# Register loads of block numbers and pair steps moved behind the last use of the numbers they replace

## The reference

```python
# layer 0: two attention convolutions over edges (src -> dst) plus one loop edge per node
xs = (x @ lin_w.T).reshape(N, H, C)                      # H = 8 heads, C = 16
alpha = a_src[src] + a_dst[dst] + a_edge                 # per edge and head
alpha = jnp.where(alpha > 0, alpha, 0.2 * alpha)
alpha = jnp.exp(alpha - segment_max(alpha, dst)[dst])
out = segment_sum(xs[src] * alpha / segment_sum(alpha, dst)[dst], dst)
h = layer_norm(elu(out + bias) + h_previous)             # twice, then a linear layer over h0, h1, h2
# a_edge comes from a small network on x[src].x[dst], |x[src]-x[dst]|^2, |x[src]|^2, |x[dst]|^2
x = _layernorm(x + layer0)
# layer 1: messages and a gated update
em = relu(layer_norm([x[src], x[dst]] @ msg_w + msg_b)) * edge_weights[:, None]
messages = segment_sum(em, dst) / (counts + 1e-8) * (counts > 0)
h_new = relu(layer_norm([x, messages] @ upd_w + upd_b))
x = _layernorm(x + gate * h_new + (1 - gate) * x)        # gate = sigmoid(x @ gate_w + gate_b)
```

## Time and profile before

| what | value |
|---|---|
| median of 3 runs | 6742.71 us |
| the profiled execution's own time | 6751.64 us |
| its span, first to last instruction | 6749.8 us |
| TensorE busy | 5088.3 us (75%) |
| VectorE busy | 4557.2 us (68%) |
| GpSimd busy | 4633.8 us (69%) |
| mean granted TensorE clock | 0.816 of full speed |
| DMA | 534.92 MB, mean 79 GB/s |

### The profile page before, as it was taken

How to read it: one execution, slowest core, us unless ns; L and a number is a source line. 1 busy time by engine, 2 the same in 40 slices (tenths; PEclk the granted TensorE clock), 3 DMA queues, 4 the chain that set the end, 5 groups by cost and what they waited for, 6 DMA issues and landing times. The chain is left out here.

```text
span 6749.8 us, 124645 instructions
## 1 busy us (share of the span) xinstructions
PE 5088.3 (75%) x33726; PEld 4548.7 (67%) x33726; DVE 4557.2 (68%) x15714; ACT 2984.2 (44%) x10333; POOL 4633.8 (69%) x4875
## 2 busy tenths in 40 slices
PE   5788888887887378888888888866666776676775
PEld 4666666676666267777777787756666666666664
DVE  5677777777777746665666666575666666666667
ACT  3344444444444322222222222255666666666666
POOL 4777777777775077777777777706777777777771
PEclk7788888888888656666666667678999999999997
DMA  8544444444443322222222222222222222222221
GB/s 174 151 115 115 114 115 115 114 113 114 115 113 84 104 61 62 63 63 63 62 63 63 62 64 63 62 85 59 54 54 54 54 54 54 54 54 54 54 54 30
DMA packets 334709, 534.92 MB, mean 79 GB/s; under 512 B 105502, under 2 KB 222767, under 8 KB 333665
## 3 DMA queue, kind: packets, MB, share of 16 engines
q0 software_dynamic: 181264, 439.20, 25.7%
q1 hardware_dynamic: 143462, 83.65, 4.6%
q10 hardware_dynamic: 9323, 4.08, 0.3%
HBM read 489.59 MB, written 42.61 MB: 79 GB/s over the span
## 5 line engine op out<-in xcount | busy, mean ns | idle before, releaser
L931 POOL DMA_INDIRECT arena<-rows,slot_src x3222 | 3086.2, 958 | 1028.1 <-issue 934.9
L723 POOL DMA_INDIRECT arena<-msg_rows,slot_src x1611 | 1523.3, 946 | 525.0 <-issue 485.5
L1129 ACT ACTIVATE arena<-psum 128x512 f32<-128x512 bf16 x808 | 480.5, 595 | 1521.4 <-PE psum L977 1518.3
L2033 PE MATMUL psum<-arena 128*128 x3232 | 700.6, 301 | 506.7 <-DMA arena<-msg_rows,slot_src 443.6
L1018 PE MATMUL psum<-arena 128*128 128x145 f32 x3232 | 978.0, 394 | 0.0
L1267 DVE TENSOR_TENSOR arena<-arena,psum 128x290 f32 x1616 | 731.3, 453 | 287.7 <-DVE arena L1267 182.3
L2033 PEld LDWEIGHTS psum<-arena 128*128 128x128 f32 x3232 | 521.3, 203 | 571.0 <-issue 570.5
L1020 PE MATMUL psum<-arena 128*128 128x145 f32 x3232 | 872.7, 361 | 0.0
L2040 ACT ACTIVATE arena<-psum 128x128 bf16<-128x128 f32 x1616 | 425.4, 277 | 753.4 <-PE psum L2035 753.0
L1204 DVE TENSOR_TENSOR arena<-arena,psum 128x512 f32<-128x512 f32 x808 | 553.5, 685 | 267.4 <-PE psum L1020 261.9
L1033 PE MATMUL psum<-arena 128*128 x3232 | 598.8, 327 | 163.7 <-ACT arena L1129 71.9
(11 more groups left out here) (360 smaller groups left out, 9567.8 us busy)
## 6 DMA issues: line engine op xcount, KB each, us to landing
arena<-rows,slot_src POOLq DMA_INDIRECT x3222
arena<-msg_rows,slot_src POOLq DMA_INDIRECT x1611
arena<-slot_keys SPq DMA_DIRECT2D x100, 128.0 KB
edge_alpha<-arena SPq DMA_DIRECT2D x50, 128.0 KB, 1.9
arena<-edge_alpha SPq DMA_DIRECT2D x50, 128.0 KB
slot_keys<-lane_keys SPq DMA_DIRECT2D x24, 256.0 KB
arena<-rows SPq DMA_DIRECT2D x6, 1024.0 KB, 10.0
rows<-arena SPq DMA_DIRECT2D x4, 822.0 KB
```

The costliest lines, as they stand in the source:

```text
L723: pool.indirect_dma_start(out=self.buffer[:, v % U, j, :], out_offset=None, in_=self.source, in_offset=bass.IndirectOffsetOnAxis(ap=K.SRC[ ...
L931: pool.indirect_dma_start(out=E.rowbuf[:, r, j, :], out_offset=None, in_=E.source, in_offset=bass.IndirectOffsetOnAxis(ap=K.SRC[:, at:at + ...
L1129: act.activation(E.onehotT[:, v % 2, :, :], E.psT, ACT.Copy).then_inc(E.turned, 1)
L2033: pe.matmul(psH[b][:, j, :], onehotT[:, b, j, :], K.by_dst[:, bass.ds(blocks(v, j), 1), :].rearrange("p b w -> p (b w)"), start=True, stop ...
```

## The change

All register loads stay, in number and content, and each moves to an earlier place in its engine's order: behind the last instruction that uses the eight numbers which it replaces, instead of in front of the first that needs the new ones. The first load of each table stands ahead of the loop.

```diff
@@ edge_pe
         v = t + 1
-        if 0 <= v < VISITS and v * G % LOADED == 0:
-            blocks = numbers_loaded(K, ET.PE, K.slot_blocks, v * G, NB - 1)
+        if v == 0:
+            blocks = numbers_loaded(K, ET.PE, K.slot_blocks, 0, NB - 1)
+            steps = numbers_loaded(K, ET.PE, K.pair_steps, 0, AW)
         near = G - 1 if E.first else G
...
             edge_select(E, v, G - 1, blocks[(v * G + G - 1) % LOADED]).then_inc(E.selected, 1)
+        if 0 <= v < VISITS - 1 and (v + 1) * G % LOADED == 0:
+            blocks = numbers_loaded(K, ET.PE, K.slot_blocks, (v + 1) * G, NB - 1)
 
         u = t + 1 - BEHIND
         if 0 <= u < VISITS:
-            if u * 2 % LOADED == 0:
-                steps = numbers_loaded(K, ET.PE, K.pair_steps, u * 2, AW)
...
                           ).then_inc(E.scattered, 1)
+            if u < VISITS - 1 and (u + 1) * 2 % LOADED == 0:
+                steps = numbers_loaded(K, ET.PE, K.pair_steps, (u + 1) * 2, AW)
@@ edge_dve
     dve, K = E.K.dve, E.K
+    blocks = numbers_loaded(K, ET.DVE, K.pair_blocks, 0, NB - 1)
...
         u = t - 17
         if 0 <= u < VISITS:
-            if u * 2 % LOADED == 0:
-                blocks = numbers_loaded(K, ET.DVE, K.pair_blocks, u * 2, NB - 1)
             for k in range(2):
                 block = blocks[(u * 2 + k) % LOADED]
...
                 edge_add(E, u, k, block)
+            if u < VISITS - 1 and (u + 1) * 2 % LOADED == 0:
+                blocks = numbers_loaded(K, ET.DVE, K.pair_blocks, (u + 1) * 2, NB - 1)
@@ message_pass
     pe_blocks[0] = numbers_loaded(K, ET.PE, K.slot_blocks, 0, NB - 1)
+    dve_blocks[0] = numbers_loaded(K, ET.DVE, K.slot_blocks, 0, NB - 1)
     for v in (0, 1):
         sums(0, v, lambda _, j: blocks_pe(v, j))
+    pe_blocks[1] = numbers_loaded(K, ET.PE, K.slot_blocks, LOADED, NB - 1)
...
-            if (at + 2) * G % LOADED == 0 and at + 2 < VISITS:
-                pe_blocks[(at + 2) * G // LOADED] = numbers_loaded(K, ET.PE, K.slot_blocks, (at + 2) * G, NB - 1)
-            if at * G % LOADED == 0:
-                dve_blocks[at * G // LOADED] = numbers_loaded(K, ET.DVE, K.slot_blocks, at * G, NB - 1)
...
                 sums(i, v + 2, lambda _, j: blocks_pe(at + 2, j))
+            if (at + 3) * G % LOADED == 0 and at + 3 < VISITS:
+                pe_blocks[(at + 3) * G // LOADED] = numbers_loaded(K, ET.PE, K.slot_blocks, (at + 3) * G, NB - 1)
             ready.wait(pe, i, v)
...
+            if (at + 1) * G % LOADED == 0 and at + 1 < VISITS:
+                dve_blocks[(at + 1) * G // LOADED] = numbers_loaded(K, ET.DVE, K.slot_blocks, (at + 1) * G, NB - 1)
```

## The result

The changed kernel takes 6816.79 us (median of 5 runs, 6809.19 to 6832.79), the kernel before 6747.60 us beside it (5 runs, 6740.57 to 6750.45): ratio 1.0106, 95% interval 1.0095 to 1.0117. It is 69 us slower. The forecast, 6890 us, had the sign and the place right and about twice the size.

The account below looks back on a forecast made before the run. GpSimd's gathers bound the messages and second pass, the TensorE-VectorE loop the first. First pass +141 us (+2.1 per period, 106, plus clock 35), second +5, messages +1, total +147: 6890 us, range 6775 to 7040.

Parts of the forecast that it names:

- New holes at u mod 8 = 2 and 6: First pass, u the visit scattered: slot loads newly between selects and scatter cost +1.0 and +1.7 us per eight visits.
- VectorE's loads: First pass: moved behind the second add, partly hidden by the mult's wait for the scatter; -0.85 and -0.37 us per period.
- the clock: First pass: more holes raise TensorE's half-speed share from 0.24 to 0.35; 0.7 us per period, 35 us (0 to 100).
- the pair-step loads: First pass: twice per period, now behind the scatter, in front of transposes and selects; 0.35 us each, +0.7 (0 to 3.8).
- the old stalls: First pass: the slot loads' stalls at their old place, mostly not reaching VectorE; -0.1 us per period (down to 0.7).
- TensorE's issue waits in front of the scatter: Sign of being right: in the first pass their count grows from 41 to over 120 in the same stretch.
- Mult waits grow from 209.8: Sign of being right: VectorE's mult waits for the scatter total more than 209.8 us in the first pass's stretch.
- Gathers further apart in the first pass only, clock under 0.88: Sign of being right: GpSimd's gathers exceed 1.276 us spacing in the first pass only, whose clock falls under 0.88.
- A, the loads hide: Rival, chance 0.10: loads disappear behind queued work, the first pass reaches GpSimd's pace and gains 41 us; 6702 us.
- The cap of 41 us: First pass: most a faster loop can win before GpSimd's 1.250 us per gather binds, 1611 gathers x 0.026.
- C, the second pass: Rival, chance 0.13: second pass's clock stays at half, TensorE becomes the bound, 141 us more; 7031 us.
- The messages: Message pass: TensorE's load moves in front of the scatter, GpSimd keeps its pace; +1 us (0 to 5) for the tail.

Follow-up runs that it names:

- e5: Kernel before with only TensorE's slot loads of the two attention passes moved behind the fourth select, undisturbed chip: 7145.12 us, ratio 1.0593.
- e8: Kernel before with pair-step loads moved behind the scatter and VectorE's loads behind the second add, slot loads unmoved, undisturbed chip: 6715.54 us, ratio 0.9957.
- e12: Changed kernel without pair-step reloads (loaded once per attention pass), chip with late releases: 8165.18 us, ratio 0.9944 to the kernel before.
- e6: Kernel before with only the pair-step loads moved behind the transposes, in front of the selects, undisturbed chip: 6713.86 us, ratio 0.9957.
- e7: Kernel before with each table loaded once per attention pass and never reloaded, so sums go to wrong blocks, undisturbed chip: 6686.94 us, ratio 0.9912.
- e11: Kernel before with only VectorE's pair-block loads moved behind the second add of the visit before, chip with late releases: 8208.14 us, ratio 0.9995.
- e1: Kernel before with only TensorE's slot loads of the attention passes moved behind the fourth select, chip with late releases: 8293.20 us, ratio 1.0090.

## Why the prediction was right in kind and twice too large

**The place.** The loop between TensorE and VectorE sets the pace of the first pass, the slot loads between selects and scatter lengthen it, the other passes don't move. All shown: by the pass lengths, by e5, and by e8, which takes the slot loads out of the change and turns +1.06% into -0.43%. How the total divides among the terms is in part bookkeeping, as said below.

**The terms.** Per period of eight visits the first pass went from 1700 / (1333 / 32) = 40.8 us to 1700 / (1280 / 32) = 42.5 us, by the 1333 and 1280 gathers in 400 to 2100: +1.7, where the prediction had +2.8. I put each mult of that stretch into its place in the period and averaged its wait, for e5 as well:

| wait of the mult for the scatter, us | u mod 8 = 0 | 1 | 2 | 4 | 6 | sum |
|---|---|---|---|---|---|---|
| before | 3.37 | 0 | 0 | 1.0 | 0.6 | 5.0 |
| after | 1.54 | 0.2 | 0.69 | 0 | 2.71 | 5.1 |
| e5 | 5.72 | 0 | 0.75 | 3.57 | 2.79 | 12.8 |

- New holes at u mod 8 = 2 and 6: predicted 1.0 + 1.7 = 2.7. The waits there rose by 0.7 and 2.1, together 2.8; in e5, where VectorE's loads are unmoved, by 0.75 and 2.2, together 2.9. Right.
- VectorE's loads: predicted -0.85 - 0.37 = -1.2. The waits at 0 and 4 fell by 1.8 and 1.0; VectorE's visible load rose from 71.8 / 41.7 = 1.7 us to 60.8 / 40 + (77.4 - 9.5) / 40 = 3.2 us, 9.5 us being what the take's issue waits were before. -2.8 + 1.5 = -1.3. Right, by the trace's accounts; no run took this edit alone on an undisturbed chip. One can read the same numbers as a rival: the mult's waits hardly changed in sum (5.0 and 5.1 us), and the 1.5 us that VectorE's load shows more are nearly all of the lengthening. For the reading by places speaks e5: its two single holes alone give 2.9 us, more than the whole 1.7, so something else in the change must win back over 1 us. That it is VectorE's load, no run on an undisturbed chip separates.
- What is left, 1.7 - 2.8 + 1.3 = +0.2 us, is the clock, the pair-step loads and the old stalls together. Predicted 0.7 + 0.7 - 0.1 = +1.3. These are the terms of the sum that were mis-sized, the pair-step loads and the clock: 1.1 us, 56 us over 50.5 periods, of the 59 us by which the first pass and its forecast differ (82 against 141).
- Of it, the clock: I let the share at half speed rise from 0.24 to 0.35; it rose to 0.28 (0.86). At my own price, 3 x 0.04 x 2.2 = 0.26 us and 13 us for the pass, not 35.
- The pair-step load, then, is left with about zero, not 0.7. That is a remainder and not a measurement. The 1.26 us hole in front of the transposes at 1514.18 is real, and in the trace ScalarE waits 1.16 us for them, until 1514.60; but the selects behind them end at 1515.61, and VectorE's take, held by its own load, starts at 1516.96. The scatter behind, for which the mult waits 2.46 us, may still come later by it. That it could be free was my lower end; e8 shows that two such loads in a period still allow a loop at GpSimd's pace, and e12 speaks for a cost in the change. It stays open.

**What the prediction asked for.** TensorE's issue waits in front of the scatter from 41 to over 120: the profile books 79 as issue and 39 on ScalarE's columns, 118 together, three in each of 40 periods; right in kind once the second row is read as what it is, and two short of the number. "Mult waits grow from 209.8": wrong in total, 205.3; the count rose from 107 to 140. I had worked out myself that VectorE's load would fill up to 0.9 us of each such wait at two places, and did not subtract it from the total. A sum of waits doesn't grow when another stall of the same engine moves into it; by place in the period it is seen. Add and rescale lost their issue waits: right. Gathers further apart in the first pass only, clock under 0.88: right.

**A, the loads hide.** The register loads mostly hide behind the transposes (27.6 us in 47 waits before), show 0.8 us behind the scatter (33.7 us in 42 in e8) and nearly whole behind the selects. The Trainium skill, "TensorE: Matmul & The Clock Gate" (Architectural detail: the array is 16× 32×32, not 1× 128×128), gives TensorE a queue of 64 instructions. The trace agrees as far as queued instructions do cover a load behind the transposes, where at most 0.8 us shows; how deep the queue is, no run here shows. Behind the selects it doesn't help: 1.72 us for one load, 3.69 for two. That this is so because the fourth select itself waits for VectorE's make is argued from the order of the program.

**The cap of 41 us.** Two errors. The first pass's floor is 1.261 to 1.263 us per gather (e6 to e8), so the pass has some 2052.4 - 2033.2 = 19 us to give. It could have been read from the earlier trace rows: a gather there lasts 749.76 / 784 = 0.956 us, in the messages 756.21 / 800 = 0.945, and the 0.011 us are nearly the whole difference of the floors. And the stretch between the last gather of the first pass and the first of the second shrinks as well, which the prediction left at nothing: 206.7 us before, 193.8 in e6 (2124.8 to 2318.6), 188.5 in e8, 183.9 in e7. A loop that keeps up has fewer visits left to work off when the last gather is issued; that reading is argued, the lengths are measured.

**C, the second pass.** Did not come: its length fell by 3 us, its clock stayed at 0.68. In e5, with twice the load in one place, it took 2025.2 us (2751.8 to 4777.0). The reason that I gave, that a TensorE which is behind hides its loads, is not what e5 shows: in 2800 to 4750 TensorE idles 124.9 us in 47 waits in front of the rescale and 81.4 us in 31 in front of the scatter, up to 3.6 us each. VectorE's wait for rows gave way, to 236.5 us in 158 waits (594.2 in 330 before), and GpSimd kept its pace. The slack of the loop took the holes, not a queue.

**The messages.** As forecast: +0.7 us where +1 was. TensorE's load now shows in front of the scatter, 64.4 us in 131 waits in 4780 to 6630, and its wait for rows fell from 410.3 to 292.1 us.

**The start.** The three loads at the head of the passes hold one of GpSimd's first gathers: it waited 9.47 us at 122.64, where it waited 2.1 us before. That TensorE's two loads stand in the way there is seen in front of its first selects, 3.68 us on "issue" where it was 1.86. The prediction had no term for it; at most 7.3 us, less what the full buffers take back.

```profile
122.64 0.95 POOL L931 DMA_INDIRECT arena<-rows,slot_src  x1 [9.47 <-PE psum L1036]
```

**A version that beats both.** e6 and e8 are such versions, by 0.43% against the kernel before and by about 1.5% (101 to 103 us of 6817) against the changed one, the two kernels before being 3 us apart.

## What to carry to other kernels

A register load held its engine's sequencer for some 1.9 us in every place that was tried (medians 1.92 us on TensorE, 1.83 on VectorE); what it costs the program is decided by what is queued in front of it and free to run, and by the slack of whoever waits behind it. Put it behind a long row of instructions that wait for nothing (here the transposes, or with a smaller hole the scatter), not between an instruction that waits for another engine (here the selects) and one that another engine waits for (here the scatter). "As early as the old numbers are dead" is no rule: of the loads moved that way in this kernel, those of slots cost 96 us (e8 against the changed kernel), which the others could not win back, their gain being capped by the next bound.

A wait's releaser is the profile's guess: if it names an engine whose work of that rank was ready a visit earlier, look for the register load in front. And when stalls move within an engine, don't judge by the total of one wait; put the waits into their place in the period.

## What the runs showed of the hardware that was not expected

Two register loads in a row leave a hole of 3.6 to 3.7 us where one leaves 1.7: they don't overlap (e5).

The same program takes 6745 us on one of the chips and 8212 to 8220 on two others, 22% more, at a clock of 0.73 to 0.74 for the whole span, with waits of up to 17 us (e11) that the profile puts to none of the core's engines. The register loads last as long there as here (1.92 us). An edit that costs 5.9% on the one (e5) costs 0.9% on the other (e1). Why these chips are so, no run shows.
